# Scores two ticks earlier in a batch, weighted values behind the logits on TensorE, norm chains spread over the slots of a tick

## What is computed

```python
x = x + attention0(groupnorm(x))        # 8 heads of 16, relative bias over time and particle, causal in time, then @ Wo
t = t + attention1(layernorm(t))        # logits[i,j] = w2 . tanh(A[i] + B[j]) + b2, softmax over j, @ V
t = t + moe(layernorm(t))               # gate softmax, top 2 of 8 experts with capacity, gelu MLP of width 512
```

## Time and profile before

| | |
|---|---|
| median of 3 runs | 2644.57 us (2638.53 to 2649.14) |
| profiled execution: own time | 2655.62 us |
| its span, first to last instruction | 2653.8 us |
| PE busy | 2138.1 us (81%) |
| DVE busy | 1744.5 us (66%) |
| ACT busy | 1694.6 us (64%) |
| POOL busy | 1527.6 us (58%) |
| mean granted TensorE clock | 0.914 of full |

### The profile page before, as it was taken

The page is one execution under the profiler, slowest core; times in us unless marked ns, Lnnn a source line. Parts: engine busy times, 40 slices in busy tenths (PEclk is TensorE's granted clock), DMA queues, the critical chain, the costliest instruction groups (busy, mean ns, idle before and its releaser), DMA issues.

```text
span 2653.8 us, 56738 instructions
## 1 busy us (share of the span) xinstructions
PE 2138.1 (81%) x17969; PEld 1145.5 (43%) x17969; DVE 1744.5 (66%) x4714; ACT 1694.6 (64%) x2003; POOL 1527.6 (58%) x1591
## 2 busy tenths in 40 slices
PE   0278998887888888888888889888988896638887
PEld 0134444443444444444444444444444443327666
DVE  5577676777776777776777677767776745423333
ACT  5023876776777677766777767677777787813333
POOL 3302655656575747474756474747475757827777
PEclk9778998999999999998999999999898998859999
DMA  5342331221313122222222222222222100014553
GB/s 138 72 88 60 55 64 30 65 39 56 50 51 50 50 46 58 43 62 44 61 44 62 45 60 44 58 45 52 45 49 38 23 11 5 6 45 78 79 79 36
DMA packets 146539, 138.22 MB, mean 52 GB/s; under 512 B 25754, under 2 KB 137127, under 8 KB 146145
## 3 DMA queue, kind: packets, MB, share of 16 engines
q1 hardware_dynamic: 120848, 110.11, 20.3%
q0 software_dynamic: 25360, 24.14, 5.4%
HBM read 82.68 MB, written 54.12 MB: 52 GB/s over the span
## 4 chain that ended last, share of the span: by engine, by line
PE 54%; DVE 20%; issue 8%; DVEq 6%; POOL 4%; DMA 3%; SPq 2%; ACT 2%; POOLq 2%; ACTq 0%
PE logits L922 17%; PE av_bank L908 5%; PE ring L994 5%; PE scores L892 4%; PE scores L895 4%; PE ring L1016 3%; DVE max_halves L1193 3%; POOL out_dram L557 3%; PE ring L979 3%; PE ring L1013 2%; DVE ln_small L1083 2%; PE ring L1008 2%; DVEq L1383 2%; PE ring L990 2%; DVE bias_q L1107 2%
## 5 line engine op out<-in xcount | busy, mean ns | idle before, releaser
L765 POOL TENSOR_SCALAR hidden<-b_rep,a_cols 128x768 f32<-128x768 f32 x1152 | 1031.5, 911 | 771.4 <-PE logits L922 585.8
L826 ACT ACTIVATE probs<-scores 128x512 f32<-128x512 f32 (+1 forms) x768 | 401.3, 545 | 673.8 <-PE scores L895 671.1
L845 ACT ACTIVATE hidden<-hidden 128x2304 f32<-128x2304 f32 x384 | 815.3, 2123 | 15.9 <-POOL hidden L765 15.9
L922 PE MATMUL logits<-hidden,w_shifted 128*32 128x384 f32 x6144 | 616.8, 523 | 53.3 <-ACT probs L833 36.2
L1193 DVE TENSOR_REDUCE max_halves<-ring 128x1 f32<-128x384 f32 (+4 forms) x896 | 472.5, 550 | 181.6 <-PE ring L994 175.4
L852 ACT ACTIVATE hidden<-b_rep,a_cols 128x768 f32<-128x768 f32 x384 | 357.9, 932 | 0.0
L994 PE MATMUL ring<-k_max,q_max 112*128 112x384 bf16 (+4 forms) x1024 | 309.7, 329 | 50.8 <-DMA k_max<-qk_parts 24.4
L922 PEld LDWEIGHTS logits<-hidden,w_shifted 128*32 128x32 f32 x6144 | 169.8, 113 | 298.4 <-issue 276.5
L892 PE MATMUL scores<-bias_q,onehot_k 96*128 96x512 bf16 (+1 forms) x768 | 287.3, 374 | 8.8 <-DMA q_parts<-max_parts 5.5
L895 PE MATMUL scores<-q_parts,k_parts 99*128 99x256 bf16 (+1 forms) x1536 | 285.6, 268 | 0.0
L908 PE MATMUL av_bank<-probs,v_aug 128*32 128x256 f32 (+1 forms) x3072 | 234.6, 379 | 0.2 <-ACT probs L826 0.2
(11 more groups left out here) (262 smaller groups left out, 2832.3 us busy)
## 6 DMA issues: line engine op xcount, KB each, us to landing
qk_parts<-qk_parts_sb SPq DMA_DIRECT2D x16, 1152.0 KB, 4.3
q_parts<-qk_parts SPq DMA_DIRECT2D x192, 96.0 KB, 3.8
k_parts<-qk_parts SPq DMA_DIRECT2D x192, 96.0 KB, 4.6
q_max<-qk_parts SPq DMA_DIRECT2D x96, 96.0 KB, 2.9
k_max<-qk_parts SPq DMA_DIRECT2D x96, 96.0 KB, 3.5
expert_rows<-probs POOLq DMA_DIRECT2D x1, 7920.0 KB
x_in<-in_x_dram SPq DMA_DIRECT2D x96, 64.0 KB, 2.2
x<-in_x_dram SPq DMA_DIRECT2D x96, 64.0 KB, 2.2
```

Of the source, the lines that this page charges most:

```text
L765: last = g.tensor_scalar(hidden[:, q % SLOTS, o, :], b_rep[:, side], 1.0, a_cols[:, side, a_col(q, o):a_col(q, o) + 1], ALU.mult, ALU.add)
L826: s.activation(probs0[:, d % 3, 2 * pair:2 * pair + 2, 0:n_], scores[:, pair].rearrange("p (j l) -> p j l", j=2)[:, :, 0:n_], ACT.Exp) \
L845: s.activation(hidden[:, t % SLOTS, 0:3, :], hidden[:, t % SLOTS, 0:3, :], ACT.Tanh)
L922: last = mm(logits[32 * g:32 * g + 32, half, 0:HALF], w2_shifted[:, k, :], hidden[:, q % SLOTS, g, HALF * half:HALF * half + HALF], start= ...
```

## The change

- **Scores.** `FILL_AT`, `EXP_AT` and `VALUES_AT` go from 36, 37, 38 to 34, 35, 36. The tables `AT` and `MAX_COUNTS` are rewritten around that.
- **PE's order in a tick.** `add_logits` for q = 4k stood at the start of tick 4k + 2, so that such a tick held two logit steps and tick 4k + 1 none. Now each tick has one: for q = 4k in slot 2 of tick 4k + 1, for the others at the tick's start. `weigh_values` stands directly behind it instead of in slot 3.
- **DVE.** `norm_scale` of `end` goes from the four slots of tick 4 to four places in ticks 4 to 6 (`NORM_AT`), and also carries the group norm's inverse root as a seventh column, whose own three Newton steps in tick 7 go. The norm of `mid` starts in tick 16 and has links with a ring read between. The gate's steps move to ticks 10 and 11, `place` and what follows to ticks 12 to 14, with `write_slots` on its own.
- **Two parts of the maximum** instead of three: two DVE operations fewer and one memset more per `maxT`, one row DMA fewer, contraction over 98 rows instead of 99.
- **`position`**: 18 matmuls instead of 37, with the right side read by broadcast. Its constants need three more selects by POOL before the passes start.
- **SP and POOL** move: `load_max_rows` from ticks 11 and 23 to 8 and 20, `load_scores` from 14 to 13, POOL's split of q and k from ticks 15, 16 to 16, 17, their store from 17 to 18.

```diff
-FILL_AT, EXP_AT, VALUES_AT = 36, 37, 38
+FILL_AT, EXP_AT, VALUES_AT = 34, 35, 36
...
-AT[5] += [("mid", "heads", 0)]
-AT[9] += [("mid", "heads", 1)]
-AT[15] += [("mid", "heads", 2)]
-AT[10] += [("mid", "headsT", 0)]
...
+AT[3] += [("mid", "heads", 0)]
+AT[7] += [("mid", "heads", 1)]
+AT[13] += [("mid", "heads", 2)]
+AT[9] += [("mid", "headsT", 0)]
...
+NORM_AT = ((4, 3), (5, 0), (5, 2), (6, 0))
...
-                    mm(bank[:, 0:n_], before_mid[:], chosen[:].rearrange("p b e -> p (b e)"), start=True, stop=False,
+                    mm(bank[:, 0:n_], before_same[:], chosen[:].rearrange("p b e -> p (b e)"), start=True, stop=False,
                        skip_group_check=True)
-                    for tb in range(TB):
-                        for other in range(TB):
-                            if other != tb:
-                                mm(bank[:, E * tb:E * tb + E], (before_le if other < tb else before_lt)[:],
-                                   chosen[:, other, :], start=False, stop=False, skip_group_check=True)
+                    for other in range(TB):
+                        mm(bank[:, 0:n_], before_lt[:], chosen[:, other, :].unsqueeze(1).to_broadcast([P, TB, E]),
+                           start=False, stop=False, skip_group_check=True)
+                    for other in range(TB - 1):
+                        later = TB - 1 - other
+                        mm(bank[:, n_ - E * later:n_], same[:],
+                           chosen[:, other, :].unsqueeze(1).to_broadcast([P, later, E]),
+                           start=False, stop=False, skip_group_check=True)
...
-                    if ps.has("end") and t == 0:
-                        add_logits(ps.batch("end"), TICKS - 1)
-                    if ps.has("add") and t % 4 == 2:
-                        add_logits(ps.batch("add"), t - 2)
-                    if ps.has("add") and t > 0 and t % 4 in (3, 0):
-                        add_logits(ps.batch("add"), t - 1)
...
-                    stage, d = score_step(t, VALUES_AT)
-                    if ps.has(stage):
-                        weigh_values(ps.batch(stage), ps.side(stage), d)
...
+                    fill_stage, step = score_step(t, FILL_AT)
+                    values_stage, weighed = score_step(t, VALUES_AT)
+                    stage, q = ("add", t - 1) if t else ("end", TICKS - 1)
+                    for slot in range(PARTS):
+                        if slot == 0 and q % 4 and ps.has(stage):
+                            add_logits(ps.batch(stage), q)
+                        if slot == 0 and q % 4 and ps.has(values_stage):
+                            weigh_values(ps.batch(values_stage), ps.side(values_stage), weighed)
+                        for use in parts[slot]:
+                            if ps.has(use[0]):
+                                fill(ps, use)
+                        if slot < 2 and ps.has(fill_stage):
+                            fill_scores(ps.batch(fill_stage), step, slot)
+                        if slot == 2 and q % 4 == 0 and ps.has(stage):
+                            add_logits(ps.batch(stage), q)
+                        if slot == 2 and q % 4 == 0 and ps.has(values_stage):
+                            weigh_values(ps.batch(values_stage), ps.side(values_stage), weighed)
...
-                            if t == 18 and slot >= 2:
+                            if t == 17 and slot >= 2:
                                 norm_scale(0, slot - 2)
-                            if t == 19 and slot < 2:
-                                norm_scale(0, slot + 2)
-                            if t == 19 and slot >= 2:
-                                if slot == 2:
+                            if t == 18 and slot in (1, 3):
+                                norm_scale(0, 2 + slot // 2)
+                            if t == 19 and slot in (1, 3):
+                                if slot == 1:
                                     dve.drain()
```

155 lines of the change are left out of this document (68 added, 87 removed).

## The result

The changed kernel takes **2724.9 us** (median of 4 runs, 2722.77 to 2730.32) where the kernel before took 2646.9 in the same comparison (2638.53 to 2650.84): ratio 1.030, 95% interval 1.027 to 1.033. It is 3% slower. The forecast was 2464 and the range 2370 to 2580, so both missed, and the sign too.

A forecast was written before the change was run, and what follows sets the result against it. PE was taken to set the pace; terms summed to -13.2 us a pass, from 136.5 to 123.3. Twelve full passes gave -158, all together -181 us, so a median of 2464 us, range 2370 to 2580.

The forecast's parts named there:

- What bounds the kernel: PE sets the pace, busy 118.8 of 136.5 us a pass; DVE, which PE waits for, is late, not full.
- Values behind the logits, -4.8: On PE, each of 24 ticks saves one exit and one entry of column groups, 0.2 us each: -4.8 us a pass.
- the slower one: Rival: PE waits for `exp_logits` every fourth tick, 8.4 us a pass, and the clock falls; about 2790 us, chance 0.04.
- The norm chains, -11: PE's waits for DVE at `x1T`, `headsT` and before `heads` shrink from 12.9 to 2 us: -11 us a pass.
- Logits of q = 4k, +3.5: One tick earlier, PE's logits wait for ACT's `exp_logits` of the same tick: +3.5 us a pass.
- Clock, -3: Half-clock stretches behind PE's long waits go; a third of 9.7 us is taken: -3 us a pass.
- The rival's clock price: In the slower case, chance 0.04, the clock falls after each `exp_logits` wait, six times, costing 15 us a pass.
- DVE in ticks 9 to 13, +2.5: q, k, gate steps, `place` and tags crowd DVE beside ring reads that PE waits for: +2.5 us a pass.
- `position`: On PE, 18 matmuls instead of 37 take 0.6 us instead of 1.01: -0.4 us a pass.
- the moved-waits rival: `x1T`, `heads`, q and k meet DVE late at new places; -6 us a pass, about 2560 us, chance 0.20.
- The values' own ends: Limits for PE's saving from values behind the logits: 0 if PE waits there anyway, and 5 us a pass.

The follow-up runs named there:

- e6: The kernel before, with DVE's max reduction reading only the first half of the keys: 2609.6 us.
- e4: The kernel before, with the values right behind the logits in 18 ticks and DVE's copy of `av_bank` in the values' own tick: 2653.8 us.
- e7: e4 with DVE's max reduction reading only the first half of the keys: 2609.0 us.
- e1: The changed kernel, with DVE's copy of `av_bank` in the tick of the values instead of the next one: 2662.5 us.
- e2: The changed kernel, with the values back behind the second score pair and slot 2's ring uses: 2597.3 us.
- e10: e2 with `maxT` of head group 1 in tick 21 instead of 20: 2586.3 us.
- e8: e2 with the logits of q = 4k back at the start of tick 4k + 2: 2607.5 us.
- e15: e2 with POOL's additions over half of the columns and ACT's tanh reading `b_rep` instead of the sums: 2437.4 us.
- e13: The changed kernel, with POOL's additions over half of the columns and ACT's tanh reading `b_rep` instead of the sums: 2535.0 us.
- e11: The kernel before, with POOL's additions over half of the columns and ACT's tanh reading `b_rep` instead of the sums: 2498.4 us.

## Why the prediction was wrong

**What bounds the kernel** was half right. DVE is late and not full: e6 shows it. But "PE sets the pace" was not: in e4 and e7 PE has 3.3 to 3.7 us less to do a pass and nothing is gained.

**Values behind the logits, -4.8.** This step failed, by its sign. On PE the saving is there: 3.3 us for 18 joins in e4. But the step asked only what the move saves on PE, and not what the moved instruction waits for. At the first step of a group (kb = 0) it waits for `av_copied`. DVE gives that at the start of the tick behind the group's last values, after everything that its tick before holds; before, PE came there only at that tick's end. That wait costs 4.4 us a pass (the change against e1), and the new place another 3.4 (e1 against e2), of which the longer waits of ring uses are the main part and the cause stays open. Net +7.8 for the 18 joins that e2 undoes, instead of -4.8 for all 24. No rival had it either: the slower one built its price on the exponential and the clock, and that its 2790 came nearest was luck.

**The norm chains, -11.** Right in direction, too large. `x1T` fell from 6.7 to 0.8 us as the change stands, but this was partly because other waits stood in front: in e2 it is 2.0, and in e10 6.2. In e2 the waits of this term's kind are 2.0 + 1.6 and the new one of `maxT` 2.8, so 6.4 of 12.9 us remain, where 2 were assumed. The links are apart now, and each can meet POOL's additions again. The prediction also read the 3.37 us stall as one with three additions; it began in the POOL instruction before them.

**Logits of q = 4k, +3.5.** The wait was sized well: 4.0 us a pass in the change, 3.8 in e2. But e8 to e2 the pass falls by 1.1 (134.6 to 133.4), with the double tick gone and six joins won, which no run parts. The term was a cost of 3.5, and no cost shows.

**Clock, -3.** Wrong. The half-clock stretches still hold 18.9 us a pass. The long waits behind which they stood went, and others came. How much PE waits in all does not set their length: between before and the change the rest grows from 18.9 to 27.5 and they stay; e10 has as much rest as e2 (17.2 and 16.8) and 12.4 us at half clock against 16.4. They are shortest where the rest is least, 4.7 in e15. The rival's clock price did not come either: the granted clock stayed at 0.93. The Trainium skill (TensorE: Matmul & The Clock Gate, "A second HAM failure mode: psum-queue depth-cycling") tells of a kernel whose frequent short idles made the clock swing. The rival took from it that more waits cost more clock; between before and the change these traces show no difference, 18.9 us at 1.2 GHz in both.

**DVE in ticks 9 to 13, +2.5.** Of that size at most: L1020 waits 2.9 us a pass in the change, 1.4 in e2, and had next to nothing before, but half of the change's 2.9 lies in tick 3 and only 1.4 in tick 11. `position` takes PE 0.60 us a pass instead of 1.08, as predicted; POOL and SP show no new wait of PE.

Without the values' move, the sum of the other terms was -8.4 a pass and e2, which keeps six joins, shows -3.1; with it, -13.2 was forecast and +4.7 came. Even the moved-waits rival assumed that the join's saving stays.

**The range** of 2370 to 2580 had an upper bound made of gains that fail to come. The values' own ends, 0 and 5 us saved, held no wait that the moved instruction brings along. In the trace of the kernel before nobody waits for the copy (L1366) in nine passes; that says there is slack, and not how much of it the move uses up.

## What to carry over

When an instruction moves earlier in its engine's queue, list the semaphores it waits on, and for each one where its signal stands in the *other* engine's order; a producer that was done half a tick early becomes the critical one when its consumer moves by half a tick. Price a saving on the busiest engine at nothing until a wait at the same place is shown to be absent. And in a chain of tiny dependent instructions count their number and what each can meet, before spreading them out: one link fewer in each was worth 45 us whichever order stood around it, while in the change, which spreads them, the stall stands at 13.2 us a pass instead of 7.9.

## What was not expected of the hardware

- A DVE product over six columns took up to 3.38 us beside POOL's sending of expert rows and three additions, and its stall ended with the third. Halving the additions took 9 to 12 us a pass off DVE's busy time and 148 to 190 us off the whole, on engines that are busy 56 to 66% of the span.
- `normed`, a DVE operation of SBUF to SBUF over 128 columns with one large input, is held up likewise: in the change 3114 ns at most against 338 in the median, with half additions (e13) 650 at most; before 1307 at most, in e11 618. By source line, changed kernel:

```profile
L1145 DVE TENSOR_SCALAR heads<-x,ln_mv,ln_small x54: 312/338/3114, 778.2 to 1917.4; 128x128 f32<-128x128 f32 x54
```
